# Between the attentions of a four-layer network: order of row reads, weight reads, FFN matmuls, rounding steps and key buffers

## Chip, cores and metric

One core of one Trainium2 chip. The metric is the device time of one execution in microseconds (us); a kernel is stated by the median of its runs. The engines are TensorE (PE), VectorE (DVE), ScalarE (ACT), GpSimd (POOL), and SyncE (SP), which here only issues DMAs.

## The reference, cut to what matters

A residual stream x of 2 x 1024 tokens and 128 features passes four layers, each with an attention and a feed-forward network (FFN) on the same normalised input:

```python
for L in range(4):
    xn = _layernorm(x)
    s = attention[L](xn)            # 0: grouped, rotary; 1: 16 heads; 2: features x features; 3: one shared head of keys
    g = _silu(ffn[L](xn))           # 0: mixture, top 2 of 8, capacity; 1: 8 small experts, all computed; 2: ternary; 3: mixture
    x = x + s * g

# layer 1's FFN
gate, up = einsum('td,edf->tef', xf, Wg), einsum('td,edf->tef', xf, Wu)
h = silu(gate) * up                 # then weighted by the router, and projected down, plus a shared expert

# layer 2's FFN; _tlin is x @ w.T * s with w in {-1, 0, 1}
h = silu(_tlin(x, w1_w, w1_s)) * _tlin(x, w2_w, w2_s)
h = gelu(_tlin(h, h1_w, h1_s), approximate=False)
h = gelu(_tlin(h, h2_w, h2_s), approximate=False)
return _tlin(h, w3_w, w3_s)
```

## The kernel before, in words

Matmuls that need more than one rounded product split an operand into a high part (rounded to the fast 32-bit format by an ACT cast) and a low part (what the cast left out, subtracted by DVE), and run three matmuls: high x high, low x high, high x low (`mm3`, L828). "Batch" below means such a group of matmuls into one PSUM bank.

All engines walk through one list of items, written out by hand in `whole_order` (L472), each taking from an item its own share of the work, and wait for each other by semaphores. An item that uses PSUM draws its bank from a pool in turn (`BANKS`, `POOLS`), so the order also fixes the banks. Engines are in order: an item that waits holds up all that stands behind it on its engine, and SP holds up every DMA behind a wait.

The list is, in time: attention 0 (to about 556 us of the trace), layer 0's experts (to about 660), attention 1 (to 1201), layer 1's FFN (to 1286), layer 2 (attention and ternary FFN interleaved, to 1464), attention 3 (to 2036), layer 3's experts. A `barrier` item stands where buffers change owners.

- **Experts** (`expert_order`, L370). Layer 0 has 16 units, two per expert, of 384 and 256 rows. For each unit `xrows` (SP) reads its rows into one of five xg buffers, `cols` transposes them, four `up` batches with gelu and one `down` follow; `ew` reads an expert's two weight matrices, `esplit` rounds the first. `xrows` of unit u + 3 stands ahead of unit u. `wld` reads the seven pieces of layer 1's weights (six of 256 KB, into the place of its values, `vt`) and `ald` its output matrix (512 KB, `wo`): all of them stand in front of unit 0.
- **Layer 1's FFN** (`first_ffn_order`, L422). Four chunks of 512 tokens, five tiles m of 128 hidden features. `f1g` is the gate batch with ACT's silu, `f1u` the up batch with DVE's product, `f1w` (m < 4) spreads the router's weights over the tile by two matmuls whose contraction has 8 rows, and DVE multiplies them in. `f1sp` splits the weights in pieces (gh/gl, then uh/ul), `f1wt` the router's weights (wth/wtl).
- **Layer 2** (`layer2_order`, L444). `f2g` is two batches, gate and up, into two banks. For each, ACT takes silu of the gate into one of three temporary tiles, DVE multiplies the up bank in, ACT casts the product to `hs` high, DVE subtracts to `hs` low; then `f2h 0` and `f2h 1` (hidden layers, 12 matmuls each per tile) and `f2d`. All of one `f2g` is one item, so on ACT the silu of the next tile stands behind the cast of this one. `a2g`, `a2t`, `a2s`, `a2sm`, `a2sn`, `a2n`, `a2m`, `a2f` are the steps of its attention, per batch of 1024 tokens; `aln0` to `aln2` its layer norm, where `aln2` scales eight tiles on DVE and then POOL; `sil` and `xup` update x. The list takes one entry of the attention's part and one of the FFN's in turn.

This is f2g on ACT before, with the product's wait (`emptied`) inside:

```python
S.activation(t[:], ps[:], AF.Silu, scale=fn.sc[:, mt:mt + 1]).then_inc(s.free[b], 1)
w.wait_ge(*pl.emptied(*item))
if ch:
    w.wait_ge(*pl.filled("f2h", 0, ch - 1, 3))
S.copy(fn.hs[0][0][:, mt, :].bitcast(FR), t[:]).then_inc(s.f2_act, 1)
```

- **Start of an attention** (`attention_order`, L239). The keys of the first heads come in two column halves, each: matmuls, ACT's cast into `stage[0]`, DVE's low part into `stage[1]`, DMAs from both into kA and kB (items `k`, `khi`, `klo`). The second half waits until the copies of the first have left the stage. The queries go the same way through `hq` (`qhi`, `qlo`). Then come the `max` items, score maxima that DVE reduces. Layer 3 has also `sn` and `snt`, scores of the null key, ahead of the first maxima. `early` reads the next FFN's first weights into the stage once the last key item's copies are through.

## Time and profile before

| | |
|---|---|
| median of 3 runs | 2091.08 us (2090.39 to 2096.55) |
| the profiled execution, its own time | 2092.04 us |
| its span in the profile | 2090.2 us |
| mean granted clock of TensorE | 0.954 of 2.4 GHz |
| layer 0's experts, 556 to 660 us | PE busy 79.4 of 104.0 us, clock 0.86 |
| layer 1's FFN, 1201 to 1286 us | PE busy 78.2 of 85.0 us, clock 0.84 |
| layer 2, 1286 to 1464 us | PE busy 156.3 of 178.0 us, clock 0.96 |
| attention 1, 660 to 1201 us | PE busy 514.4 of 541.0 us, clock 0.97 |

How to read it: the span runs from the first to the last instruction, and the execution's own time is 1.84 us more. "Busy" of PE counts an instruction from its start to its end, at whichever clock it ran; a stretch can be fully busy at half the clock. In a row of a timeline the square brackets hold the time for which the engine did nothing before it, and what ended that.

### The profile page before, as it was taken

To read this page: it belongs to the slowest core of one execution; us is meant where nothing else is said; L and a number is where in the kernel's file an instruction comes from. 1 tells how busy PE (TensorE), PEld (TensorE's weight loads), DVE (VectorE), ACT (ScalarE), POOL (GpSimd) and SP (SyncE) were. 2 spreads that over 40 slices of the span, in tenths; PEclk is the share of its full clock that TensorE was granted. 3 is DMA by queue.
4 is the path that set the end of the run, shared out by engine and by line. 5 is a ranking of instruction groups with operands and counts; after the bars stand their busy time and mean duration, and the time that the engine had idled before them with its cause. 6 is when DMAs were issued, how large, how long until landed. Compare 5 with 4: busy or idle time off the path is not lost.

```text
span 2090.2 us, 31314 instructions
## 1 busy us (share of the span) xinstructions
PE 1891.8 (91%) x9714; PEld 1247.0 (60%) x9714; DVE 1381.0 (66%) x3813; ACT 965.5 (46%) x2003; POOL 1230.7 (59%) x1600
## 2 busy tenths in 40 slices
PE   5899999999885899999999898988889999888985
PEld 3565556665584566666666566876556655545554
DVE  7887777777343776666666455446688888766733
ACT  2435444444454554555545434545335444444443
POOL 1668977777544367777777700011367777788743
PEclk9999999999897899999999979999799999999997
DMA  5336132132152433443444120000312223222233
GB/s 143 93 86 156 45 82 53 35 73 51 53 161 68 104 80 88 105 101 79 105 98 96 38 84 20 1 12 1 91 41 67 64 58 74 66 67 69 59 106 100
DMA packets 125966, 155.54 MB, mean 74 GB/s; under 512 B 21880, under 2 KB 66200, under 8 KB 125544
## 3 DMA queue, kind: packets, MB, share of 16 engines
q1 hardware_dynamic: 121704, 145.42, 28.1%
q0 software_dynamic: 4096, 8.12, 1.2%
q8 instruction: 78, 1.28, 0.3%
q14 instruction: 88, 0.72, 0.1%
HBM read 47.84 MB, written 17.40 MB: 31 GB/s over the span
## 4 chain that ended last, share of the span: by engine, by line
PE 59%; POOL 11%; DVE 11%; issue 11%; ACT 4%; DMA 1%; SPq 1%; POOLq 0%; DVEq 0%; ACTq 0%
PE P L826 58%; POOL acc L1583 4%; DVE P L1974 2%; POOL yd L1600 2%; POOL pr L1561 2%; POOL xg L1591 2%; POOL acc L1580 2%; ACT pr L1347 1%; DVE mx L1963 1%; DVE mx L1984 1%; DMA xg<-xs,sidx 1%; PE P L912 1%; DVE qB L1936 1%; DVE bst L1875 0%; PE P L853 0%
## 5 line engine op out<-in xcount | busy, mean ns | idle before, releaser
L1583 POOL TENSOR_TENSOR acc<-acc,pr 128x512 f32<-128x512 f32 (+3 forms) x768 | 677.0, 904 | 61.4 <-ACT pr L1347 37.1
L1347 ACT ACTIVATE pr<-P 128x512 f32<-128x512 f32 (+1 forms) x768 | 396.0, 567 | 314.5 <-PE P L826 307.5
L826 PE MATMUL P<-pr,vt 128*64 128x512 f32 (+3 forms) x2304 | 431.4, 499 | 17.6 <-POOL pr L1561 16.9
L826 PE MATMUL P<-qA,kA 128*128 128x512 f32 (+2 forms) x1024 | 395.5, 390 | 27.7 <-ACT pr L1347 23.8
L1561 POOL TENSOR_SCALAR_AFFINE_SELECT pr<-pr 128x256 f32<-128x256 f32 x384 | 156.7, 408 | 367.0 <-ACT pr L1347 261.2
L826 PE MATMUL P<-qB,kB 128*128 128x512 f32 (+2 forms) x1024 | 368.3, 366 | 0.0
L826 PE MATMUL P<-kA,qA 128*128 128x512 f32 (+2 forms) x1152 | 313.2, 374 | 17.7 <-DMA qA<-hq 4.8
L826 PEld LDWEIGHTS P<-qA,kA 128*128 128x128 f32 x1024 | 194.4, 190 | 153.2 <-issue 73.4
L1963 DVE TENSOR_REDUCE mx<-P 128x1 f32<-128x512 f32 x384 | 244.7, 683 | 57.3 <-PE P L826 55.7
L826 PEld LDWEIGHTS P<-pr,vt 128*64 128x64 f32 x2304 | 141.5, 137 | 221.1 <-issue 148.7
L826 PEld LDWEIGHTS P<-kA,qA 128*128 128x128 f32 x1152 | 194.0, 195 | 125.9 <-issue 72.0
L1974 DVE CUSTOM_DVE_ANT_0 P<-P,maskQ 128x128 f32<-128x128 f32 (+3 forms) x384 | 178.2, 519 | 102.3 <-PE P L826 101.2
L1580 POOL TENSOR_TENSOR acc<-pr,pr 128x384 f32<-128x384 f32 x192 | 217.8, 1146 | 32.6 <-ACT pr L1347 32.4
L826 PEld LDWEIGHTS P<-qB,kB 128*128 128x128 f32 x1024 | 195.1, 190 | 21.3
L1974 DVE CUSTOM_DVE_ANT_0 P<-P,maskQ,mx 128x128 f32<-128x128 f32 (+3 forms) x384 | 188.6, 553 | 11.6 <-PE P L826 9.0
L1342 ACT ACTIVATE pr<-P 128x512 f32<-128x512 f32 x192 | 86.2, 488 | 134.9 <-PE P L826 131.4
L826 PE MATMUL P<-xh,weights 128*128 128x512 f32 (+2 forms) x336 | 114.9, 425 | 9.9 <-DVE stage L1944 4.4
L2021 DVE SCALAR_TENSOR_TENSOR P<-P,rd 128x512 f32<-128x512 f32 x96 | 66.5, 693 | 81.4 <-ACT rd L1360 81.4
L1600 POOL DMA_INDIRECT yd<-y,ni x64 | 62.3, 973 | 90.2 <-DVE y L2252 67.7
L826 PE MATMUL P<-acc,ones 128*64 128x512 f32 x384 | 104.4, 622 | 8.9 <-POOL acc L1583 5.3
L1974 DVE DVE_READ_ACCUMULATOR2_ANT mx<- 128x1 f32 x768 | 107.3, 140 | 0.3
L826 PE MATMUL P<-wo,z 128*128 128x128 f32 x768 | 98.1, 282 | 7.4 <-DVE z L2028 7.4
(345 smaller groups left out, 2705.9 us busy)
## 6 DMA issues: line engine op xcount, KB each, us to landing
qA<-hq SPq DMA_DIRECT2D x384, 128.0 KB
kA<-stage SPq DMA_DIRECT2D x168, 128.0 KB
qB<-qB SPq DMA_DIRECT2D x96, 128.0 KB
kB<-stage SPq DMA_DIRECT2D x84, 128.0 KB, 2.4
nr<-null_share SPq DMA_DIRECT2D x64, 128.0 KB
yd<-in_c_zero SPq DMA_DIRECT2D x32, 128.0 KB, 2.7
w<-in_L_W SPq DMA_DIRECT2D x16, 256.0 KB, 5.7
xg<-xg SPq DMA_DIRECT2D x24, 129.0 KB
```

The source lines that it names most:

```text
L826: return P.matmul(out, lhs, rhs, start=start, stop=stop)
L912: P.transpose(ps[0:72, 0:128], m.A[L].mx[pl.chunk(*k) % 2][:], m.ident[:]).then_inc(s.full[b], 1)
L1342: S.activation(a.pr[slot][:, :, 512 - wide:512], src, AF.Exp, scale=0.125).then_inc(s.free[b], 1)
L1347: S.activation(a.pr[slot][:, r, 512 - wide:512], m.bank[b][:, 512 - wide:512], AF.Exp, scale=0.125).then_inc(s.free[b], 1)
L1561: G.affine_select(tile, tile, [[0, 2], [1, 128]], ALU.is_ge, 0.0, 0, -1).then_inc(s.sel, 1)
L1580: G.tensor_tensor(acc[:, sl], p0[:, sl], pt[:, sl], ALU.add).then_inc(s.acc, 1)
L1583: G.tensor_tensor(acc[:, sl], acc[:, sl], pt[:, sl], ALU.add).then_inc(s.acc, 1)
L1591: G.indirect_dma_start(xgd[L], bass.IndirectOffsetOnAxis(ap=r.sidx[:, i // 2, i % 2:i % 2 + 1], axis=0), r.xs[i % 2][:], None).then_inc(s. ...
L1600: G.indirect_dma_start(yd[L], bass.IndirectOffsetOnAxis(ap=e.ni[u % 4][0:wide, t:t + 1], axis=0), e.y[u % 4][0:wide, t, :], None).then_inc ...
L1963: V.reduce_max(mx[:, 8 + j:9 + j], ps[:, 0:wide], X).then_inc(s.free[b], 1)
L1974: top = V.tensor_tensor_reduce(tile, tile, m.maskQ[:, 512 - wide:512], 1.0, least, ALU.add, ALU.max, mx[:, j:j + 1])
L2021: chain(V.scalar_tensor_tensor(out=m.bank[b][:], in0=m.bank[b][:], scalar=-1.0, in1=y[:], op0=ALU.mult, op1=ALU.mult))
```

## The change

1. Layer 0's experts: `xrows` of units 2 and 3 stand ahead of the first weights, and later ones four units ahead instead of three. The seven `wld` and the `ald` of layer 1 stand one in each of units 0 to 6 (the last with `ald`).
2. Layer 1's FFN: the first chunk begins gate 0, gate 1, up 0, gate 2, up 1. At the barrier before it, ACT loads the table of activations for silu.
3. Layer 2: cast and low part of `f2g` are an item of their own, `f2c`, placed one tile later; `sil` and `xup` of layer 1's last chunk stand ahead of the first `f2g`; the attention's steps stand two entries later, and `aln2` of batch 0 behind `a2n`, `a2m` of batch 1.
4. The second key item of each attention goes through two of the buffers `z`, with semaphores of its own. Layer 3's `sn` stands behind the first maxima.

```diff
@@ attention_order @@
-    if L == 3:
-        od.add("sn", L, 0)
     for g in range(10):
...
-        if L == 3 and g == 1:
-            od.add("snt", L, 0)
+        if L == 3 and g < 2:
+            od.add(("sn", "snt")[g], L, 0)
@@ expert_order @@
+    ahead = 4 if L == 0 else 3
     if L == 0:
-        od.add("xrows", L, 2)
+        od.extend([("xrows", L, 2), ("xrows", L, 3)])
     od.extend([("ew", L, 0), ("ew", L, 1), ("esplit", L, 0), ("cols", L, 0), ("ew", L, 2)])
-    if L == 0:
-        od.extend([("wld", 1, i) for i in range(len(PIECES[1]))] + [("ald", 1)])
     for u in range(n):
-        if u + 3 < n:
-            od.add("xrows", L, u + 3)
+        if u + ahead < n:
+            od.add("xrows", L, u + ahead)
+        if L == 0 and u <= len(PIECES[1]):
+            od.add(*(("wld", 1, u) if u < len(PIECES[1]) else ("ald", 1)))
@@ first_ffn_order @@
     for ch in range(4):
+        if ch == 0:
+            od.extend([("f1g", 0, 0), ("f1g", 0, 1), ("f1u", 0, 0), ("f1g", 0, 2), ("f1u", 0, 1)])
         for m in range(5):
-            od.extend([("f1g", ch, m), ("f1u", ch, m)])
+            od.extend([it for it in (("f1g", ch, m), ("f1u", ch, m)) if it not in od.place])
@@ layer2_order @@
-    od.extend([("a2s", 0), ("f2g", 0, 0), ("f2g", 0, 1), ("sil", 1, 3), ("xup", 1, 3), ("f2g", 0, 2), ("f2g", 0, 3), ("ln1", 2, 1), ("lnr", 2, 1), ("a2sm", 0, 0), ("a2sm", 0, 1),
+    od.extend([("a2s", 0), ("sil", 1, 3), ("xup", 1, 3), ("f2g", 0, 0), ("f2g", 0, 1), ("f2c", 0, 0), ("f2g", 0, 2), ("f2c", 0, 1), ("f2g", 0, 3), ("f2c", 0, 2),
+               ("f2c", 0, 3), ("ln1", 2, 1), ("lnr", 2, 1), ("a2sm", 0, 0), ("a2sm", 0, 1),
...
-    att = [[], [("xT", 2, 2)], [("xT", 2, 3)], [("a2g", 1)], [("a2t", 1)]] + rest(0) + out(0)[:2] + [[("a2s", 1)]] + out(0)[2:] + [[("a2sm", 1, 0), ("a2sm", 1, 1), ("aln1", 0)]]
-    att += [[("a2sn", 1, 0)], [("a2sn", 1, 1)]] + scale(0) + rest(1) + [[("wld", 3, i)] for i in range(3)] + [[("nld",)]]
+    att = [[], [("xT", 2, 2)], [("xT", 2, 3)], [("a2g", 1)], [("a2t", 1)], [], []] + rest(0) + out(0)[:2] + [[("a2s", 1)]] + out(0)[2:] + [[("a2sm", 1, 0), ("a2sm", 1, 1), ("aln1", 0)]]
+    att += [[("a2sn", 1, 0)], [("a2sn", 1, 1)]] + rest(1) + scale(0) + [[("wld", 3, i)] for i in range(3)] + [[("nld",)]]
-    gate = lambda ch: [[("f2g", ch, m)] for m in range(4)]
+    gate = lambda ch: [[("f2g", ch, m)] + [("f2c", ch, n) for n in ((), (0,), (1,), (2, 3))[m]] for m in range(4)]
@@ Plan @@
+    def second_keys(self, L, b, kp, c):
+        return [x for x in self.key_items if x[0] == L].index((L, b, kp, c)) == 1
+    def key_stage(self, m, *k):
+        return m.A[k[0]].z[2:4] if self.second_keys(*k) else m.stage
@@ scalar_program @@
             if kind == "barrier":
+                if k[0] == 2:
+                    S.preload_act_table_set("silu_and_others")
...
-                w.wait_ge(*pl.emptied(*item))
+            elif kind == "f2c":
+                ch, mt = k
+                gate = ("f2g",) + k
+                t = m.F2.tmp[(od.step[gate] + 1) % 3]
+                b2, uses2, _ = od.bank[gate][1]
+                w.wait_ge(s.free[b2], uses2 + 1)
                 if ch:
                     w.wait_ge(*pl.filled("f2h", 0, ch - 1, 3))
@@ vector_program @@
+            elif kind == "f2c":
+                ch, mt = k
+                f2, n = m.F2, od.step[("f2g",) + k]
+                t = f2.tmp[(n + 1) % 3]
                 w.wait_ge(s.f2_act, n)
                 V.tensor_tensor(f2.hs[0][1][:, mt, :].bitcast(FR), t[:], f2.hs[0][0][:, mt, :], ALU.subtract).then_inc(s.f2_lo, 1)
```

Where the order moves, as it stands on the engines. On SP at the start of layer 0's experts, first before, then now (xg are rows, w and w1raw the experts' weights, vt the first pieces of layer 1's):

```order
L1636 DMA xg_105<-xg 128x2x129
L1638 DMA xg_105<-xg 128x129
L1771 DMA w_100<-in_L_W 128x4x128
L1771 DMA w_101<-in_L_W 128x4x128
L1768 DMA w1raw_89<-in_L_W 128x512
L1771 DMA w_102<-in_L_W 128x4x128
L1673 DMA vt_167<-in_L_Wq 128x512 x2
L1673 DMA vt_167<-in_L_Wk 128x512 x2
L1673 DMA vt_167<-in_L_Wv 128x512 x2
L1687 DMA wo<-in_L_Wo 128x8x128
L1636 DMA xg_106<-xg 128x2x129
```

```order
L1656 DMA xg_105<-xg 128x2x129
L1658 DMA xg_105<-xg 128x129
L1656 DMA xg_106<-xg 128x2x129
L1791 DMA w_100<-in_L_W 128x4x128
L1791 DMA w_101<-in_L_W 128x4x128
L1788 DMA w1raw_89<-in_L_W 128x512
L1791 DMA w_102<-in_L_W 128x4x128
L1656 DMA xg_107<-xg 128x2x129
L1658 DMA xg_107<-xg 128x129
L1693 DMA vt_167<-in_L_Wq 128x512
L1788 DMA w1raw_90<-in_L_W 128x512
L1791 DMA w_103<-in_L_W 128x4x128
```

The rows of unit 3 (xg_106) stood behind all reads for layer 1; now they stand ahead of every weight, those of unit 4 (xg_107) ahead of the first read for layer 1, and one such read comes with each unit.

On PE at the start of layer 1's FFN, before and now (gh, gl and uh, ul are high and low part of gate and up weights, wth and wtl the router's weights):

```order
L826 MATMUL P<-xl,gh 128x512
L826 MATMUL P<-xh,uh 128x512
L826 MATMUL P<-xh,ul 128x512
L826 MATMUL P<-xl,uh 128x512
L826 MATMUL P<-wth,selr 128x512
L826 MATMUL P<-wtl,selr 128x512
L826 MATMUL P<-xh,gh 128x512
```

```order
L839 MATMUL P<-xh,uh 128x512
L839 MATMUL P<-xh,ul 128x512
L839 MATMUL P<-xl,uh 128x512
L839 MATMUL P<-xh,gh 128x512
L839 MATMUL P<-xh,gl 128x512
L839 MATMUL P<-xl,gh 128x512
L839 MATMUL P<-xh,uh 128x512
L839 MATMUL P<-xh,ul 128x512
L839 MATMUL P<-xl,uh 128x512
L839 MATMUL P<-wth,selr 128x512
L839 MATMUL P<-wtl,selr 128x512
L839 MATMUL P<-wth,selr 128x512
```

The second fence begins after two gate batches. The first f1w, which followed the first gate and the first up batch, now follows five batches of 128 rows, and the second f1w comes right behind it.

On ACT at layer 2's start, before and now (ftmp and the two stage tiles are the temporary tiles of f2g; L1487 is its silu, L1491 its cast, now L1502 and L1511; xf is `sil`):

```order
L1487 ACTIVATE ftmp<-P,sc 128x512
L1491 CAST hs_318<-ftmp 128x512
L1487 ACTIVATE stage_15<-P,sc 128x512
L1491 CAST hs_318<-stage_15 128x512
L1440 ACTIVATE xf<-xf 128x512
L1487 ACTIVATE stage_16<-P,sc 128x512
L1491 CAST hs_318<-stage_16 128x512
L1487 ACTIVATE ftmp<-P,sc 128x512
L1491 CAST hs_318<-ftmp 128x512
```

```order
L1455 ACTIVATE xf<-xf 128x512
L1502 ACTIVATE ftmp<-P,sc 128x512
L1502 ACTIVATE stage_15<-P,sc 128x512
L1511 CAST hs_318<-ftmp 128x512
L1502 ACTIVATE stage_16<-P,sc 128x512
L1511 CAST hs_318<-stage_15 128x512
L1502 ACTIVATE ftmp<-P,sc 128x512
L1511 CAST hs_318<-stage_16 128x512
L1511 CAST hs_318<-ftmp 128x512
```

Each cast now stands behind the silu of the next tile, and `sil` ahead of them all.

## Rows read from the trace of the kernel before

**Rows 1.** The page, part 1: busy us, share of the span, instructions.

```profile
PE 1891.8 (91%) x9714; PEld 1247.0 (60%) x9714; DVE 1381.0 (66%) x3813; ACT 965.5 (46%) x2003; POOL 1230.7 (59%) x1600
```

**Rows 2.** Windows, layer 0's experts: length, busy PE, PEld, DVE, ACT, POOL, PEclk, DMA, GB/s.

```profile
580.00:585.00 5.00, 1.41 (x5) 1.41 (x6) 0.28 (x1) 0.68 (x2) 2.81 (x3) 0.57 1.09 320
585.00:590.00 5.00, 5.00 (x31) 5.00 (x31) 1.41 (x6) 2.53 (x5) 0.00 (x0) 0.75 0.57 176
```

**Rows 3.** Timeline, layer 0's experts: start, us, what; then the issue of one pair.

```profile
574.89 1.87 SPq L1636 DMA_DIRECT2D xg<-xg  x1
...
583.59 0.69 PE L1046 MATMUL P<-ident,xg 128*128 128x128 f32 x2 [5.24 <-issue]
...
vt<-in_L_Wv SPq DMA_DIRECT2D x2, 256.0 KB, 7.7
```

**Rows 4.** Timeline, first FFN: start us, us, what, idle before it and releaser.

```profile
1202.95 0.77 PE L826 MATMUL P<-xh,gh 128*128 128x512 f32 x1 [2.32 <-DVE gl L2281]
...
1205.60 0.79 PE L826 MATMUL P<-xh,uh 128*128 128x512 f32 x1 [1.03 <-DVE ul L2281]
...
1207.61 1.28 ACT L1465 ACT_TABLE_LOAD   x1
...
1208.36 0.79 PE L826 MATMUL P<-wth,selr 8*128 8x512 f32 x1 [1.12 <-DVE wtl L2286]
...
1209.51 0.80 PE L826 MATMUL P<-xh,gh 128*128 128x512 f32 x1
...
1225.00 0.63 PE L826 MATMUL P<-xh,gh 128*128 128x512 f32 x1
```

**Rows 5.** Windows, first FFN and fourth chunk of the ternary FFN.

```profile
1220.00:1225.00 5.00, 5.00 (x12) 3.02 (x11) 1.38 (x2) 1.14 (x2) 0.00 (x0) 0.50 0.01 3
1225.00:1230.00 5.00, 5.00 (x18) 3.09 (x17) 2.77 (x4) 1.19 (x2) 0.00 (x0) 0.92 0.01 2
1240.00:1245.00 5.00, 5.00 (x22) 3.13 (x21) 3.14 (x5) 2.30 (x4) 0.00 (x0) 1.00 0.00 0
1410.00:1415.00 5.00, 3.24 (x11) 1.46 (x10) 3.25 (x5) 2.64 (x5) 0.00 (x0) 1.00 0.00 0
```

**Rows 6.** Timeline, start of layer 2: fourth tile and first hidden matmuls.

```profile
1297.32 0.68 ACT L1487 ACTIVATE ftmp<-P,sc 128x512 f32<-128x512 f32 x1
...
1298.11 0.75 DVE L2317 SCALAR_TENSOR_TENSOR ftmp<-P,sc,ftmp 128x512 f32<-128x512 f32 x1
1298.89 0.62 ACT L1491 CAST hs<-ftmp 128x512 fp32r<-128x512 f32 x1 [0.89 <-DVE ftmp L2317]
...
1299.54 0.69 DVE L2320 TENSOR_TENSOR hs<-ftmp,hs 128x512 fp32r<-128x512 f32 x1 [0.68 <-ACT hs L1491]
...
1300.34 7.59 PE L826 MATMUL P<-hs,hw 128*128 128x512 f32 x24 [5.78 <-issue]
```

**Rows 7.** Timeline, second batch of layer 2's attention.

```profile
1364.53 1.16 PE L826 MATMUL P<-wvT,ab 128*128 128x129 f32 x8 [1.22 <-DVE ab L2386]
...
1368.98 2.08 DVE L1902 TENSOR_SCALAR sacc<-sacc,mv,vb 128x128 f32<-128x128 f32 x4
...
1374.57 2.05 PE L826 MATMUL P<-weights,va 128*128 128x128 f32 x8 [4.63 <-DVE va L2358]
```

**Rows 8.** Timeline, after the fourth chunk's gates.

```profile
1430.52 0.69 ACT L1510 ACTIVATE h<-P,sc 128x512 f32<-128x512 f32 x1
...
1431.26 3.02 PE L826 MATMUL P<-hs,hw 128*128 128x512 f32 x12 [2.10 <-ACT h L1510]
```

**Rows 9.** Timeline, second keys of layers 0, 1 and 3.

```profile
31.19 0.58 ACT L1305 CAST stage<-P 128x512 fp32r<-128x512 f32 x1 [3.55 <-DVE P L1928]
...
682.51 0.58 ACT L1305 CAST stage<-P 128x512 fp32r<-128x512 f32 x1 [0.57 <-DMA kB<-stage]
...
683.24 0.59 SPq L1708 DMA_DIRECT2D qB<-qB  x1
...
1473.99 1.14 PE L826 MATMUL P<-xh,weights 128*96 128x512 f32 x2 [4.44 <-DVE stage L1944]
```

More of the change, by code:

```diff
@@ L714, in signals @@
     s.zx, s.zy = {0: one("zx0"), 3: one("zx3")}, {0: one("zy0"), 3: one("zy3")}
[L715 removed]
+    s.q_dup, s.q_low, s.q_max, s.keys_a, s.keys_b = some("q_dup", 3), some("q_low", 3), some("q_max", 3), some("keys_a", 2), some("keys_b", 2)
     s.disp, s.x_rows, s.nul_in = some("disp", 2), some("x_rows_", 5), one("nul_in")
@@ L769, in weighed, with keys_copied, keys_there @@
         return self.emptied("pv", L, b, p, c, 0)
-    def keys_copied(self, n):
-        heads = sum(1 if x[0] == 3 else 2 for x in self.key_items[:n])
+    def keys_copied(self, n, second=False):
+        heads = sum(1 if x[0] == 3 else 2 for x in self.key_items[:n] if self.second_keys(*x) == second)
         return 32 * heads, 16 * heads
-    def keys_there(self, L, b, h, part):
-        return self.keys_copied(self.od.nth("khi", L, b, h // 2 if L != 3 else 0, part))
+    def keys_there(self, s, L, b, h, part):
+        item = L, b, h // 2 if L != 3 else 0, part
+        second = self.second_keys(*item)
+        upper, lower = self.keys_copied(self.od.nth("khi", *item), second)
+        return (s.keys_a[second], upper), (s.keys_b[second], lower)
     def key_item_before(self, L, b, kp, c):
@@ L1299, in run @@
                 src = m.bank[od.bank[("k",) + k][-1][0]]
-                if pl.key_item_before(*k):
+                if pl.key_item_before(*k) and not pl.second_keys(*k):
                     w.wait_ge(*pl.emptied("k", *pl.key_item_before(*k)))
-                if n > 1:
-                    w.wait_ge(s.keys_a, pl.keys_copied(n - 1)[0])
-                    w.wait_ge(s.keys_b, pl.keys_copied(n - 1)[1])
-                S.copy(m.stage[0][0:wide, :].bitcast(FR), src[0:wide, :]).then_inc(s.k_hi, 1)
+                if n > 1 and not pl.second_keys(*k):
+                    w.wait_ge(s.keys_a[0], pl.keys_copied(n - 1)[0])
+                    w.wait_ge(s.keys_b[0], pl.keys_copied(n - 1)[1])
+                S.copy(pl.key_stage(m, *k)[0][0:wide, :].bitcast(FR), src[0:wide, :]).then_inc(s.k_hi, 1)
             elif kind == "v" and k[0] == 1:
@@ L1719, in run @@
                     for slot, rows in heads:
-                        Y.dma_start(a.kA[0:64, slot, cs], m.stage[0][rows, :]).then_inc(s.keys_a, 16)
+                        Y.dma_start(a.kA[0:64, slot, cs], pl.key_stage(m, *k)[0][rows, :]).then_inc(s.keys_a[second], 16)
                 else:
@@ L1723, in run @@
                     for slot, rows in heads:
-                        Y.dma_start(a.kA[64:128, slot, cs], m.stage[1][rows, :]).then_inc(s.keys_a, 16)
+                        Y.dma_start(a.kA[64:128, slot, cs], pl.key_stage(m, *k)[1][rows, :]).then_inc(s.keys_a[second], 16)
                     for slot, rows in heads:
-                        Y.dma_start(a.kB[64:128, slot, cs], m.stage[0][rows, :]).then_inc(s.keys_b, 16)
+                        Y.dma_start(a.kB[64:128, slot, cs], pl.key_stage(m, *k)[0][rows, :]).then_inc(s.keys_b[second], 16)
             elif kind == "rows":
@@ L1941, in run @@
                 w.wait_ge(s.k_hi, od.nth("khi", *k))
-                if n > 1:
-                    w.wait_ge(s.keys_a, pl.keys_copied(n - 1)[0])
-                V.tensor_tensor(m.stage[1][0:wide, :].bitcast(FR), m.bank[b][0:wide, :], m.stage[0][0:wide, :], ALU.subtract).then_inc(s.free[b], 1)
+                hi, lo = pl.key_stage(m, *k)
+                if n > 1 and not pl.second_keys(*k):
+                    w.wait_ge(s.keys_a[0], pl.keys_copied(n - 1)[0])
+                V.tensor_tensor(lo[0:wide, :].bitcast(FR), m.bank[b][0:wide, :], hi[0:wide, :], ALU.subtract).then_inc(s.free[b], 1)
             elif kind == "v" and k[0] != 1:
```

15 lines of the change are left out of this document (7 added, 8 removed).

## The prediction

> **What bounds the kernel.** I read the page first: TensorE (PE) is busy for 1891.8 of 2090.2 us [rows 1], so a saving counts only where it takes an idle stretch, or a stretch at the lower clock, from PE. The table of windows then shows where these lie: inside the attentions PE is busy at full clock, so the change, which touches only what lies between them, has to be paid for by four short places. I went through each with the timeline of all engines, reading for every idle time of PE what ended it. "Half" and "full" below are the two levels of its clock, 1.2 and 2.4 GHz.
>
> **Layer 0's experts.** The row read of unit 3 (xg) is issued at 574.89, behind the seven reads of layer 1's weights, whose last pair lands after 7.7 us; unit 3's transposes start at 583.59, after 5.24 us of idleness [rows 3]. "Issue" as the releaser there means that the page knows no engine for it; the read is what is late. The window from 580 to 585 has a clock of 0.57 and the next 0.75 [rows 2]: PE came back at half and reached full near 587.5, so 3.8 us of work ran at half and lost 1.9 us. The change asks for unit 3's rows before any weight and puts one weight read into each unit. The row read then has only three reads of biases and unit 2's rows ahead of it. The term is 5.2 + 1.9 = **7.1 us**. What can be late next is a weight of an expert behind one more row read; a row read of 0.13 MB takes 0.4 us at the 320 GB/s of that window [rows 2], which the lower bound covers. Bounds: 4 us (another, shorter stall appears, clock falls all the same) and 8 us. The seven issues are moved, not added; SP has the time.
>
> **Start of the first FFN (layer 1).** PE stands for 1.03 us before the first up matmul (for ul) and 1.12 us before the first f1w (for wtl) [rows 4]. Now two more gate batches and one more up batch, which need neither, stand in those places: 2.15 us gone. The preloaded activation table takes 1.28 us [rows 4] out of ACT's queue ahead of the first silu; PE did not wait for that silu, so I cost it at nothing, but it is what keeps ACT ahead now: without it the banks of the first gates would come free 1.3 us later, when PE already wants them for f1w.
> The larger term is the clock. From 1209.51 to 1225.00 [rows 4] PE worked without a gap and yet at 0.50; it rose only inside the next window [rows 5], right after two gate-and-up pairs that have no f1w between them (the fifth tile of a chunk has none). Everywhere before that a pair was followed by f1w's two matmuls, which fill only 8 of 128 rows. After 583.59 the clock rose within 3.9 us of gapless full-row work [rows 2, 3]. The new order opens, at the 1202.95 of the first gate batch [rows 4], with five batches (gate, gate, up, gate, up): fifteen full-row matmuls, 6.3 us at the 12 in 5 us of the window at half [rows 5]. I take it that the clock rises 5 us into them, near 1208. From there the chunk, which without it would end at 1225.0 - 2.15 = 1222.85, has 14.9 us of half-clock work left; 12 matmuls in 5 us against 22 in the window at full clock [rows 5] make that 8.1 us, a gain of 6.8, with the waits 8.9. Against that stands that two f1w batches now come back to back, and the clock may fall for a while after them; falling and rising again as after 583.59, 3.8 us of stretch at half twice over, would cost some 4 us. Even odds on it: **7.0 us** for waits and clock. Bounds: 2.2 (it never rises earlier) and 9.5.
> The Trainium skill speaks against this reading: its page "TensorE: Matmul & The Clock Gate" (Part 1: The HAM clock gate) says that a sustained busy engine is what lifts the throttle and that the hardware doesn't count instructions. By that rule the kind of matmul would not matter and the order would bring its waits alone, 2.2 us. This trace does not agree with it: PE was gapless for 15 us at 0.50 [rows 4, 5].
>
> **Start of layer 2.** PE ends the fourth gate pair at 1294.56 and idles 5.78 us until the low part of the fourth tile is there [rows 6]. Before, each tile went silu (0.68), product (0.75), cast (0.62) in one ACT item, so that ACT stood still for the product of the same tile and the next silu waited; the sil and xup of chunk 3 were in between as well. Now the cast is its own item one tile later, and sil/xup run ahead, under the last down and a2s matmuls. Then only the last tile's own chain follows PE: its silu starts as its gate bank is done, one up batch (three matmuls, 0.7 us) before 1294.56, near 1293.9; the product ends 0.75 after the up bank, 1295.4 with the engines' gaps; cast 0.62 and subtraction 0.69 end at 1296.8. PE starts 3.5 us earlier. Its 24 matmuls took 7.59 us, because the clock had fallen; at full they would take 5.6, but the layer norm's chain of DVE and ACT behind the casts moves by 3.5 only, so I add 0.6: **4.1 us** (bounds 2.5 and 5.5).
> **Second batch of its attention.** PE waited 4.63 us for the copies of a2n, which stood on DVE behind aln2's scalings (2.08 us for four of them beside POOL), and came back at half [rows 7]. These now come later, under the hidden layer's matmuls. But a2sn(1) is now behind the product of f2g(2,0), which waits for a silu that stands behind two table loads, and a2n cannot start before it: it was 1.22 us late [rows 7], and I estimate 4 (the product's and the normalisation's 2 us on top of the old wait and more). The one stall is traded for the other: **1.0 us** (bounds -3 and 4).
> **Fourth chunk's gates and after.** PE idles 1.76 us in the window from 1410 to 1415, about 0.3 more before the next matmuls, and 2.10 at 1431.26, where it waits for a gelu that ACT could give only at 1430.52, behind two table loads and the norm [rows 5, 8]. With the casts out of the silus' way and the norm's load no longer ahead of the first silu, the banks come free about a tile sooner and the gelu some 5 us sooner. I take nearly all of the 4.2 us, **3.8 us** (bounds 1 and 5). What is late next is the low part of layer 2's last hidden tiles on DVE.
>
> **Second keys through z.** Layer 0: ACT's second cast waited for DVE's rotation sum, not for the key copies: nothing. Layer 1: it waited for the copy at 682.51, but SP is issuing copies without a break up to 683.24 and later, and the keys' copies come behind these [rows 9]: nothing. Layer 3: PE stood 4.44 us for DVE's second stage, which only frees the bank of sn [rows 9]; now the first maxima come first, and they wait for the query copies, which move by nothing, while sn's matmuls are pushed behind them: I put it at **0** (bounds -1 and +2).
>
> **The sum.** 7.1 + 7.0 + 4.1 + 1.0 + 3.8 = 23.0 us off the profiled execution's 2092.04: 2069.0. The median of the runs, 2091.08, is 0.96 below that execution: **2068.1 us**. The measurement can tell 0.3% (6.3 us) from no change.
>
> **Rivals.**
> - The clock stays at half through the first chunk, or falls back at once: the first FFN gives 2.2 instead of 7.0, 2072.9 us. For it: one sight of a rise behind pairs is little. Against: rows 2 and 5 together. 0.2.
> - Layer 2's waits are only passed on: DVE has the same work, and a2n, a2m and the norm wait in another order. The start keeps its 4.1, the second batch loses 3 and the end gains 1: 6.8 us less than forecast, 2074.9. For it: DVE and ACT have few gaps there. 0.15.
> - Slower: the weight reads, one per unit, arrive in front of row reads and starve the experts one unit after another, as unit 3 was starved: 7.1 us each time. The first term goes, and from the third such unit on (3 x 7.1 = 21.3 against the other 15.9) it is slower; with four, 2103.6. Against: already in the window from 585 to 590 the DMA share was down to 0.57, with experts' reads running [rows 2], so one more read per unit has room. 0.02.
> - The rows of layer 0's experts come no earlier, since the reads queue in another place, and the rest is refilled within each place: at most the 2.2 and 1 of plain waits, 2088, so that the change doesn't do what it says. 0.03 with what is left over. Against: the order of issue on SP, which alone delayed that read [rows 3].
> The forecast has 0.6.
>
> **How the numbers follow.** The range takes the forecast's own bounds (2061 to 2073 for most of them together) and the first two rivals: 2059 to 2078. Faster by over 0.3% is all but the last two: 0.95; within 0.3%: 0.03; slower: 0.02.
>
> **What would show it.** Right: no idle time before unit 3's transposes and a clock of 1.0 from 574 on; ul and wtl gone from PE's waits and a clock of 1.0 before 1215 in the old count; the wait before the first hs matmuls near 2.3 us; no 2 us wait for a gelu. Wrong: new waits of PE on DMA between 580 and 610; the clock at 0.5 up to the fifth tile; a wait of PE for ab above 4 us with a2m no earlier.

## The result, and the profile after

| | before | after |
|---|---|---|
| median of the timed runs | 2090.73 us (4 runs, 2087.49 to 2096.55) | 2067.63 us (4 runs, 2066.22 to 2069.05) |
| ratio | | 0.9886, 95% interval 0.9863 to 0.991 |
| the profiled execution | 2092.04 us, span 2090.2 | 2066.22 us, span 2064.4 |
| mean granted clock | 0.954 | 0.962 |

The forecast was 2068.1 us in a range of 2059 to 2078: 0.5 us off. The terms behind it did less well: one was far too small, one too large, and the clock, which differs between profiles of equal work, took its part (below). In the page, PE's busy time falls by 11.7 us against [rows 1], so about half of the 25.8 us between the profiled executions is idle time of PE and half is work that ran at full clock instead of half:

```profile
PE 1880.1 (91%) x9714; PEld 1244.2 (60%) x9714; DVE 1382.7 (67%) x3813; ACT 966.3 (47%) x2004; POOL 1232.8 (60%) x1600
```

**Layer 0's experts**, against [rows 2, 3]: two windows, then PE's first transposes of unit 3 and SP's issue of the rows of unit 6 ahead of a read for layer 1. The transposes have no bracket: PE did not wait.

```profile
575.00:580.00 5.00, 5.00 (x45) 4.97 (x44) 1.50 (x9) 2.65 (x8) 0.00 (x0) 1.00 1.11 331
580.00:585.00 5.00, 5.00 (x41) 5.00 (x40) 2.54 (x9) 3.60 (x9) 3.25 (x3) 1.00 1.09 336
```

```profile
579.12 0.46 SPq L1656 DMA_DIRECT2D xg<-xg  x1
579.45 0.38 PE L1059 MATMUL P<-ident,xg 128*128 128x128 f32 x2
579.62 1.48 SPq L1693 DMA_DIRECT2D vt<-in_L_Wk  x1
```

**First FFN**, against [rows 4, 5]: windows, then PE's timeline. The waits for ul and wtl are gone. A matmul of 512 columns follows the one before after 0.42 us up to 1199.31 and after 0.23 us from 1199.61 on: the clock rose 5.5 us after the first gate batch. A later wait of 2.24 us, for a silu, was there before too.

```profile
1195.00:1200.00 5.00, 5.00 (x14) 3.42 (x12) 2.18 (x4) 3.37 (x7) 0.00 (x0) 0.56 1.02 306
1200.00:1205.00 5.00, 5.00 (x22) 3.05 (x21) 3.98 (x7) 1.93 (x5) 0.00 (x0) 1.00 1.05 357
```

```profile
1193.86 0.77 PE L839 MATMUL P<-xh,gh 128*128 128x512 f32 x1 [2.32 <-DVE gl L2302]
...
1198.89 0.63 PE L839 MATMUL P<-xl,gh 128*128 128x512 f32 x1
1199.31 0.46 PE L839 MATMUL P<-xh,uh 128*128 128x512 f32 x1
1199.61 0.39 PE L839 MATMUL P<-xh,ul 128*128 128x512 f32 x1
1199.84 0.40 PE L839 MATMUL P<-xl,uh 128*128 128x512 f32 x1
1200.17 0.49 PE L839 MATMUL P<-wth,selr 8*128 8x512 f32 x1
...
1247.32 0.79 PE L839 MATMUL P<-wth,selr 8*128 8x512 f32 x1 [2.24 <-ACT sg L1480]
```

**Layer 2**, against [rows 6 to 8]: every wait of PE of over 0.5 us between the fourth tile's gates and attention 3. The start waits 2.35 instead of 5.78; va is no longer waited for (4.63 before); the wait for ab grew from 1.22 to 1.88. Around the fourth chunk it now waits 1.92 for a silu and 2.97 for a low part.

```profile
1279.90 7.34 PE L839 MATMUL P<-hs,hw 128*128 128x512 f32 x24 [2.35 <-issue]
1343.57 1.16 PE L839 MATMUL P<-wvT,ab 128*128 128x129 f32 x8 [1.88 <-DVE ab L2411]
1387.60 7.77 PE L839 MATMUL P<-hs,hw 128*128 128x512 f32 x33 [1.92 <-ACT stage L1502]
1413.48 4.60 PE L839 MATMUL P<-hs,hw 128*128 128x512 f32 x12 [2.97 <-DVE hs L2351]
1428.16 3.81 PE L839 MATMUL P<-w,h 128*128 128x128 f32 x32 [0.98 <-ACT h L1530]
```

In the kernel before, PE's waits around that chunk were smaller and more, beside the 2.10 of [rows 8]:

```profile
1410.98 0.50 PE L826 MATMUL P<-xh,tw 128*128 128x512 f32 x1 [0.53 <-ACT ftmp L1487]
...
1413.59 0.73 PE L826 MATMUL P<-xh,tw 128*128 128x512 f32 x2 [0.78 <-ACT stage L1487]
1415.29 10.92 PE L826 MATMUL P<-hs,hw 128*128 128x512 f32 x47 [0.74 <-DVE stage L2317]
...
1443.84 3.02 PE L826 MATMUL P<-hs,hw 128*128 128x512 f32 x12 [0.56 <-DVE hs L2326]
```

The 2.97 us are DVE's: the null key of layer 3 (`null`, L2018 to L2025, 6.9 us from its first row to its last) stands ahead of the low parts. DVE in the changed kernel:

```profile
1404.75 0.68 DVE L2018 TENSOR_TENSOR weights<-weights,weights 128x512 f32<-128x512 f32 x1
...
1411.45 0.17 DVE L2025 TENSOR_TENSOR weights<-weights,weights 128x16 fp32r<-128x16 f32 x1
1411.54 0.68 DVE L2351 TENSOR_TENSOR hs<-stage,hs 128x512 fp32r<-128x512 f32 x1
1412.14 0.68 DVE L2351 TENSOR_TENSOR hs<-ftmp,hs 128x512 fp32r<-128x512 f32 x1
1412.74 0.68 DVE L2351 TENSOR_TENSOR hs<-stage,hs 128x512 fp32r<-128x512 f32 x1
```

Every kernel of this study has the same stages, so the length of a stage can be compared over all profiles. PE's timeline gives it, from the first matmul of a stage to the first of the next, in us. (Layer 2 is counted from the last down matmul of the first FFN on.)

| kernel | attention 0 | experts 0 | attention 1 | first FFN | layer 2 | attention 3 |
|---|---|---|---|---|---|---|
| before | 553.9 | 104.5 | 532.0 | 82.4 | 178.4 | 555.4 |
| after | 554.9 | 96.6 | 529.2 | 74.5 | 166.6 | 560.0 |
| x1_experts | 554.3 | 98.1 | 531.1 | 82.5 | 179.1 | 559.9 |
| x2_ffn1 | 553.1 | 103.5 | 529.2 | 74.3 | 179.0 | 554.9 |
| x3_layer2 | 554.6 | 103.9 | 528.8 | 81.3 | 166.5 | 557.2 |
| x4_keys | 554.4 | 104.0 | 531.4 | 82.5 | 178.4 | 556.0 |
| x5_rows128 | 554.5 | 104.5 | 531.7 | 75.6 | 178.7 | 555.3 |
| x6_between | 554.8 | 96.8 | 531.6 | 75.6 | 167.0 | 555.3 |
| x7_f2c | 553.2 | 105.3 | 529.0 | 76.1 | 171.4 | 557.5 |
| x8_att | 554.1 | 104.2 | 532.1 | 76.1 | 176.0 | 557.7 |
| x10_nokeys | 553.7 | 96.7 | 530.2 | 71.0 | 166.6 | 555.6 |
| x11_rows | 554.5 | 98.5 | 531.7 | 81.1 | 179.2 | 555.1 |
| x9_later | 554.7 | 96.5 | 528.8 | 70.7 | 161.6 | 558.2 |
| x12_later_nokeys | 554.9 | 99.4 | 529.1 | 70.6 | 161.6 | 555.2 |

Two things are to be seen. The stages that a part of the change touches fall into groups (experts 103.5 to 105.3, then 96.5 to 99.4). And the attentions differ by 2 to 5 us between kernels whose instructions there are the same: one profile pair can't show a term of that size in them.

### The profile page after: what moved, and what is told of

Its sections match the earlier page's. It is cut to its first block, busy times and chain, and to the rows that moved or that the text cites. A ratio compares the mean times of both kernels' runs of the same rounds, so it can differ in the third digit from the quotient of the medians.

```text
span 2064.4 us, 31306 instructions
## 1 busy us (share of the span) xinstructions
PE 1880.1 (91%) x9714; PEld 1244.2 (60%) x9714; DVE 1382.7 (67%) x3813; ACT 966.3 (47%) x2004; POOL 1232.8 (60%) x1600
## 4 chain that ended last, share of the span: by engine, by line
PE 60%; DVE 12%; POOL 12%; issue 10%; ACT 4%; DMA 2%; SPq 1%; POOLq 0%; DVEq 0%; ACTq 0%
PE P L839 58%; POOL acc L1603 4%; POOL yd L1620 3%; DVE P L1995 2%; POOL pr L1581 2%; POOL acc L1600 1%; POOL xg L1611 1%; ACT pr L1362 1%; DVE mx L1984 1%; DVE mx L2005 1%; DMA xg<-xs,sidx 1%; PE P L925 1%; DVE qB L1956 1%; PE P L866 0%; DVE bst L1895 0%
## 5 line engine op out<-in xcount | busy, mean ns | idle before, releaser
L839 PE MATMUL P<-kA,qA 128*128 128x512 f32 (+2 forms) x1152 | 313.8, 375 | 26.7 <-DMA qA<-hq 11.8
L839 PE MATMUL P<-acc,ones 128*64 128x512 f32 x384 | 105.3, 627 | 8.9 <-POOL acc L1603 5.3
```

The source lines that it names most:

```text
L839: return P.matmul(out, lhs, rhs, start=start, stop=stop)
```

## Experiments

### The four parts, each alone

x1_experts is before with the expert part of the diff:

```diff
-        od.add("xrows", L, 2)
+        od.extend([("xrows", L, 2), ("xrows", L, 3)])
-        od.extend([("wld", 1, i) for i in range(len(PIECES[1]))] + [("ald", 1)])
+        if L == 0 and u <= len(PIECES[1]):
+            od.add(*(("wld", 1, u) if u < len(PIECES[1]) else ("ald", 1)))
```

> Only the change in layer 0's experts (row reads of units 2 and 3 ahead of the weights, one read for layer 1 per unit). Theory, from the two traces: the row read alone held unit 3, and with it goes the stretch at half clock behind it: about 8 us off the kernel before (between the first transposes and the last expert's matmuls the changed kernel gained 8.0), no idle time before unit 3's transposes. Rival A: only the plain wait of 5.2 us goes and the clock falls elsewhere: 5 us. Rival B: part of it comes from what the other parts do (semaphores, buffers): 3 us or less.

Measured: 2083.55 us against 2090.16 of before beside it, ratio 0.9969 (0.9957 to 0.998); 6.6 us, with an interval of 4.2 to 9.0. That alone would not tell the theory (8) from rival A (5). The profile does: the experts take 98.1 us, there is no wait before unit 3's transposes, and the clock is full from 574 to the last expert's matmuls, so it did not fall elsewhere.

x2_ffn1 has the first FFN's part:

```diff
+        if ch == 0:
+            od.extend([("f1g", 0, 0), ("f1g", 0, 1), ("f1u", 0, 0), ("f1g", 0, 2), ("f1u", 0, 1)])
+                if k[0] == 2:
+                    S.preload_act_table_set("silu_and_others")
```

> Only the change at the start of layer 1's FFN (five batches before the first f1w, table loaded at the barrier). Theory of the clock: 8.5 us off the kernel before, as the changed kernel gained between its first gate batch and 1266; granted clock 1.00 from about 10 us after the first gate batch on, against 25 us before. Rival (the order brings only its waits, and the clock rises for another reason): 2.2 us, and a clock at half up to the fifth tile.

Measured: 2082.82, ratio 0.9964 (0.9951 to 0.9977); 7.3 us. The clock was full 5.4 us after the first gate batch. The rival, 2.2, is outside the interval (0.9977 is 4.8 us).

x3_layer2 has the layer 2 part:

```diff
+    gate = lambda ch: [[("f2g", ch, m)] + [("f2c", ch, n) for n in ((), (0,), (1,), (2, 3))[m]] for m in range(4)]
+    att += [[("a2sn", 1, 0)], [("a2sn", 1, 1)]] + rest(1) + scale(0) + [[("wld", 3, i)] for i in range(3)] + [[("nld",)]]
...
```

> Only layer 2 (f2c as its own item, sil and xup first, attention's steps two entries later, aln2 moved). Theory, from the traces: 11.5 us off the kernel before (3.1 at the start, 8.2 from there to the barrier). Rival (as predicted): 8.9, with the second batch worth 1 and the fourth chunk 3.8. If layer 2 gains only because the FFN before it ended at another clock: under 6.

Measured: 2078.41, ratio 0.994 (0.992 to 0.9959); 11.8 us. The rival's 8.9 is just inside that interval (8.6 to 16.7), so the stage has to decide: layer 2 took 166.5 us, 11.9 less, and that behind a first FFN in the old order, which rules out the third possibility.

x4_keys has the keys and sn:

```diff
+    def key_stage(self, m, *k):
+        return m.A[k[0]].z[2:4] if self.second_keys(*k) else m.stage
+            od.add(("sn", "snt")[g], L, 0)
```

> Only the second keys through z and sn behind the first maxima. Theory, from the traces: attention 1 gains 2.4 us between its first transposes and its 60th us, since the second cast no longer waits for the copies of the first; attention 0 nothing; attention 3 loses about 0.8 (its first key x query matmul waits 5.6 us for a copy where the old order waited 4.4 for DVE): 1.6 off the kernel before. Rival (as predicted): 0, and the 2.4 us in attention 1 come from what stands on SP or DVE behind the experts. Second rival: the 2.5 us that attention 0 and the 3 us that attention 3 took longer in the changed kernel belong to this part and not to chance: it is then 3 us slower.

Measured: 2091.37, ratio 1.0009 (0.9997 to 1.0021), no difference that can be told from noise: the interval runs from 0.6 us faster to 4.4 slower, so the second rival, 3 us slower, is not excluded by it. What the expectation took for a gain in attention 1 was none: x2_ffn1, whose attention 1 is that of before, has it as well. Windows there of before, of x2_ffn1 and of x4_keys (length, busy PE, PEclk, DMA, GB/s):

```profile
685.00:690.00 5.00, 4.67 (x15) 0.65 0.87 203
690.00:695.00 5.00, 4.29 (x11) 0.50 0.41 93
```

```profile
685.00:690.00 5.00, 4.41 (x13) 0.66 0.78 180
690.00:695.00 5.00, 4.26 (x16) 1.00 0.03 2
```

```profile
685.00:690.00 5.00, 3.40 (x12) 1.00 0.86 200
690.00:695.00 5.00, 3.44 (x12) 1.00 0.23 53
```

Between short waits the clock is at half in one profile and full in another. The profile of before shows a slow start of attention 1.

The four medians add up to 6.6 + 7.3 + 11.8 - 1.2 = 24.5 us; together the parts gave 23.1. Within the intervals they add.

### What holds the clock down in the first FFN

x5_rows128, on the kernel before; it leaves out the router's weighting of the first chunk:

```diff
-                mm(ps[:], f.selr[:, mt, :].bitcast(FR), f.wth[:, tk].bitcast(FR), True, False)
+                lh, rh, rl = (f.gh[:, mt * 128:mt * 128 + 128], m.xh[:, tk], m.xl[:, tk]) if ch == 0 else (f.selr[:, mt, :], f.wth[:, tk], f.wtl[:, tk])
+                mm(ps[:], lh.bitcast(FR), rh.bitcast(FR), True, False)
```

> The kernel before, but in the first chunk of layer 1's FFN the two matmuls of each f1w multiply the gate weights (128 rows) with xh and xl instead of the router's weights (8 rows) with selr; they fill the same bank, take 512 columns each and wait for the same things. So the router's weighting of that chunk is left out. Theory of the clock (matmuls of 8 rows between the others hold it at half): it rises within some 7 us of the start of the gapless stretch at 1209.5, before 1217 instead of at 1226, and the kernel gains 4 to 5 us. Rival (the kind of matmul does not matter): half clock up to 1225, time unchanged within 1 us.

Measured: 2083.34 against 2089.5, ratio 0.9967 (0.9954 to 0.998); 6.2 us faster, with an interval of 4.2 to 9.6. PE still waited 0.97 for ul and 1.45 for wtl; its windows:

```profile
1205.00:1210.00 5.00, 2.65 (x5) 0.50 0.99 326
1210.00:1215.00 5.00, 5.00 (x17) 0.70 1.07 365
1215.00:1220.00 5.00, 5.00 (x26) 1.00 0.30 96
```

The clock rose 4.0 us into the gapless stretch (at 1213.0), 9.7 us after the first gate batch, where in the profile of before it took 17 (from the first f1w at 1208.36). But this one profile shows nothing by itself: x7_f2c and x8_att below keep the 8-row matmuls and rose 9.4 and 9.2 us after the first gate batch. What counts is the median. The edit also changed more than the rows. Around an f1w the matmuls of before start 0.55 to 0.60 us apart, though the profile shows no idle time, and elsewhere 0.43:

```profile
1211.81 0.63 PE L826 MATMUL P<-xl,uh 128*128 128x512 f32 x1
1212.36 0.79 PE L826 MATMUL P<-wth,selr 8*128 8x512 f32 x1
1212.96 0.62 PE L826 MATMUL P<-wtl,selr 8*128 8x512 f32 x1
1213.51 0.80 PE L826 MATMUL P<-xh,gh 128*128 128x512 f32 x1
1214.11 0.63 PE L826 MATMUL P<-xh,gl 128*128 128x512 f32 x1
```

In x5_rows128 they start 0.43 apart throughout. By these steps the four f1w of the chunk are worth 2.1 us at most without any change of the clock (an estimate: 0.6 us for each of three, 0.3 for the first, all at half). The rival, with this added, is still below the interval, so replacing the 8-row matmuls does bring the clock up earlier on the whole. Whether the 8 rows themselves hold it down, or the wider steps around them, or the other operands, no run separates. By the rule of the Trainium skill's "TensorE: Matmul & The Clock Gate" (Part 1: The HAM clock gate), as the prediction applied it, the clock of this kernel would have been that of before, and no more than the 2.1 us would have come off; the medians do not agree with that.

x6_between, on the changed kernel:

```diff
-            od.extend([("f1g", 0, 0), ("f1g", 0, 1), ("f1u", 0, 0), ("f1g", 0, 2), ("f1u", 0, 1)])
+            od.extend([("f1g", 0, 0), ("f1g", 0, 1), ("f1u", 0, 0), ("f1w", 0, 0), ("f1g", 0, 2), ("f1u", 0, 1)])
```

> The changed kernel, but the first f1w stands between up 0 and gate 2, and the second behind up 1, so that again no more than three batches come without one. Theory of the clock: the rise comes later, not before the fifth tile, some 20 us after the first gate batch, and 4 to 6 us of the changed kernel's gain of 7 in this place are lost: near 2073. Rival (only the missing waits mattered): the clock rises as in the changed kernel, 2067.6 within 1.5, or 1 us more if the first f1w waits for wtl again.

Measured: 2069.23, ratio 0.9899 (0.9882 to 0.9916). A miss for the theory as I had put it, and within what the rival gave: PE waited 0.93 for wtl and ran gate 2 and up 1 at half, and then the clock rose, 9.3 us after the first gate batch and behind a single pair:

```profile
1200.00:1205.00 5.00, 4.07 (x9) 0.50 1.05 352
1205.00:1210.00 5.00, 5.00 (x21) 0.99 0.78 270
```

The profiles of the seven kernels with the old order show that a single one proves little here. From the first gate batch to the rise of the granted clock it took 22.9 (before), 22.7 and 23.0 us (x1, x4), 19.3 and 19.2 (x3, x11), but 9.4 and 9.2 in x7_f2c and x8_att, where the clock rose behind the second pair. In x3 and x11 it rose behind the fourth pair, ahead of the fifth tile. So even with 8-row matmuls after every pair a pair can lift the clock. After an early rise the first FFN takes 76.1 us and not 81 to 82.5. With five batches in a row the clock rose within 4.1 to 5.9 us in all five profiles (after, x2, x9, x10, x12). By the stage's length the 74.4 us of after and x2 are 7.6 below the five with a late rise and 1.7 below the two with an early one.

That this varies from one execution to the next is the simplest reading, but it is not shown. The four kernels that ran together, x5 to x8, all rose early in their profiles, and those with the old order that ran at other times all rose late. If the time of the runs were the cause, before too would have been some 6 us faster beside these four. Its median there was 2089.5 us, against 2090.2 and 2091.0 at the other times.

The new order has its own fall. In x9_later and x12_later_nokeys (below) the clock fell again for 3.4 us behind the first three f1w, two of which stand back to back, while PE had no idle time. Windows of x9_later (length, busy PE, PEclk, DMA, GB/s):

```profile
1200.00:1205.00 5.00, 5.00 (x16) 0.69 1.06 362
1205.00:1210.00 5.00, 5.00 (x19) 0.97 0.19 57
```

It had risen at 1198.5, was at half from 1201.9 to 1205.3, and rose again. That costs 1.7 us. In after, x2 and x10, with the same order, it stayed full.

### Layer 2's two halves

x7_f2c is x3_layer2 with the attention's steps as before (the two empty entries behind `a2t` of batch 1 are gone too). x8_att is x3_layer2 with the old start and each cast directly behind its product:

```diff
-    att += [[("a2sn", 1, 0)], [("a2sn", 1, 1)]] + rest(1) + scale(0) + [[("wld", 3, i)] for i in range(3)] + [[("nld",)]]
+    att += [[("a2sn", 1, 0)], [("a2sn", 1, 1)]] + scale(0) + rest(1) + [[("wld", 3, i)] for i in range(3)] + [[("nld",)]]
```

```diff
-    gate = lambda ch: [[("f2g", ch, m)] + [("f2c", ch, n) for n in ((), (0,), (1,), (2, 3))[m]] for m in range(4)]
+    gate = lambda ch: [[("f2g", ch, m)] + [("f2c", ch, m)] for m in range(4)]
```

> Of the layer 2 part only f2c as its own item and the order at the start (sil and xup first); the attention's steps and aln2 stand as before. Theory: 3.1 at the start stay; in the second batch the wait for va (4.6 us) stays, since aln2 is ahead of a2n on DVE; the small waits there and in the fourth chunk go: 5 to 6 us off the kernel before. Rival (the split is all of it): 12. Second rival (nothing but the start): 3.

> Of the layer 2 part only the attention's steps two entries later and aln2 of batch 0 behind a2n and a2m of batch 1; every cast stands directly behind its product and the start is as before. Theory: the wait of 4.6 us for va goes with the clock that fell behind it, 6 us off the kernel before, the start gives nothing. Rival (the two need each other, since without the split the silus come as late as before): 3 or less.

Measured: x7_f2c 2081.03 against 2089.5, ratio 0.9964 (0.9952 to 0.9977), layer 2 171.4 us, that is 7.0 less than before: somewhat more than the theory, far from the 12 of its rival, and 3.7 of it at the start. x8_att 2088.16, ratio 0.9993 (0.9982 to 1.0004), layer 2 176.0, 2.4 less: the theory's 6 us did not come, the rival holds. (In both profiles the first FFN had its early rise, 6 us that belong to neither part.) PE's waits, first of x7_f2c, then of x8_att:

```profile
1350.88 1.16 PE L827 MATMUL P<-wvT,ab 128*128 128x129 f32 x8 [1.22 <-DVE ab L2396]
...
1360.06 2.05 PE L827 MATMUL P<-weights,va 128*128 128x128 f32 x8 [4.30 <-DVE va L2368]
...
1415.22 8.46 PE L827 MATMUL P<-hs,hw 128*128 128x512 f32 x36 [2.41 <-ACT h L1516]
```

```profile
1359.02 2.09 PE L827 MATMUL P<-wvT,ab 128*128 128x129 f32 x8 [3.25 <-DVE ab L2396]
...
1406.75 8.41 PE L827 MATMUL P<-hs,hw 128*128 128x512 f32 x29 [2.88 <-ACT stage L1488]
...
1433.47 4.62 PE L827 MATMUL P<-hs,hw 128*128 128x512 f32 x12 [2.27 <-DVE hs L2336]
```

The later steps alone remove the wait for va and bring a longer one for ab, and the two late ones in the fourth chunk. The split alone leaves va. Together they give 11.8, which is 2.4 more than the sum of 7.0 and 2.4: with the split, ab is waited for 1.88 only, 1.4 us less than in x8_att. There DVE, on its way from the product to a2sn, waits for the cast and subtracts the low part:

```profile
1355.73 0.75 DVE L2323 SCALAR_TENSOR_TENSOR stage<-P,sc,stage 128x512 f32<-128x512 f32 x1 [1.06 <-ACT stage L1488]
1357.16 0.69 DVE L2330 TENSOR_TENSOR hs<-stage,hs 128x512 fp32r<-128x512 f32 x1 [0.68 <-ACT hs L1497]
1357.89 0.42 DVE L2394 TENSOR_REDUCE sm<-ab 64x4 f32<-64x256 f32 x1
```

The other 1.0 us of the 2.4 is not traced.

### Rows or weights

x11_rows, on the kernel before:

```diff
-        od.add("xrows", L, 2)
+        od.extend([("xrows", L, 2), ("xrows", L, 3)])
-        if u + 3 < n:
-            od.add("xrows", L, u + 3)
+        if u + ahead < n:
+            od.add("xrows", L, u + ahead)
```

> The kernel before with the row reads of layer 0's experts ahead (units 2 and 3 before the weights, then four units ahead), but all reads for layer 1 still in front of unit 0. Theory (the row read of unit 3 alone was late): the experts' stage takes 97 to 98 us as with the whole edit, against 103.5 to 105.3 in the kernels with the old order, and 7 us come off. Rival (spreading the weights is what helps, since the third and fourth expert's weights stand behind them): a new wait of 2 us or more for w or w1raw between 590 and 615, and 3 us or less off.

Measured: 2082.66 against 2091.0, ratio 0.9961 (0.9949 to 0.9973). The experts take 98.5 us; one wait for rows of 0.70 us is left, at 583.96, and none for a weight. The rival, 3 us or less, is outside the interval (5.6 to 10.7). Asking for the rows first is nearly all of it; by the stage, 98.5 us against a mean of 97.4 with the whole edit, spreading the weights is worth about 1 us.

### Keys once more, and what was late next

x10_nokeys takes the keys and sn back out of the changed kernel:

```diff
-        return m.A[k[0]].z[2:4] if self.second_keys(*k) else m.stage
+                    for slot, rows in heads:
+                        Y.dma_start(a.kA[0:64, slot, cs], m.stage[0][rows, :]).then_inc(s.keys_a, 16)
```

> The changed kernel with the keys and sn as they were before. Theory (the second keys through z are worth nothing, what the attentions differ by is the clock): within 1.5 us of the changed kernel's 2067.6, either way. Rival 1 (the new buffers serve the start of attention 1): 2 to 3 us slower. Rival 2 (they cost in attentions 0 and 3): 2 to 5 us faster.

Measured: 2064.13 against 2091.0, ratio 0.9878 (0.986 to 0.9895); that interval and the changed kernel's overlap. Its first FFN was 3.5 us shorter than the changed kernel's although the order there is the same: after the wait of 2.25 us for a silu at 1246 its clock stayed full, where the changed kernel's fell (0.72 and 0.60 in the windows from 1245 to 1255). Of the twelve kernels with this wait it is the only one whose clock did not fall there.

x9_later is the changed kernel with three steps later:

```diff
-    att += out(1) + [[("aln1", 1)], []] + scale(1) + [[("wsp", 3, i)] for i in range(3)] + [[("null", 3)]]
+    att += out(1) + [[], [], [("aln1", 1)], []] + scale(1) + [[("wsp", 3, i)] for i in range(3)]
-                ("f2h", 1, 3, 0): [("xT", 3, 0)], ("f2h", 1, 3, 1): [("xT", 3, 1)]}
+                ("f2h", 1, 3, 0): [("xT", 3, 0)], ("f2h", 1, 3, 1): [("xT", 3, 1), ("null", 3)]}
-                od.extend([("ln1", 2, 0), ("lnr", 2, 0)])
+                od.extend([("ln1", 2, 0)])
-                od.extend([("ln2", 2, 0)])
+                od.extend([("lnr", 2, 0), ("ln2", 2, 0)])
```

> The changed kernel with three steps that need not be done where they stand put later: the null key (6.7 us of DVE) behind xT 3 1, where DVE has 8.8 us without work; aln1 of batch 1 two entries later, so that ACT's change of tables comes after the last silus of the fourth chunk; lnr of layer 2's first half behind the gate of tile 2 instead of tile 1 in the last chunk of the first FFN. Theory: the waits of PE at 1387.60 (1.92, for a silu), 1413.48 (2.97, for a low part) and part of that at 1247.32 (2.24, for a silu) go, with half a clock stretch each time: 4 to 7 us off the changed kernel, near 2062. Rival (each wait comes back at the next thing that is late): within 2 us of the changed kernel.

Measured: 2058.13 us (2054.49 to 2058.37), ratio 0.9843 (0.9827 to 0.9858). It is 9.5 us below the changed kernel by the medians and 9.0 by the two ratios, more than the 4 to 7 expected, and the rival is out. All of PE's waits of over 0.5 us from the middle of the first FFN to attention 3:

```profile
1276.38 7.34 PE L839 MATMUL P<-hs,hw 128*128 128x512 f32 x24 [2.35 <-issue]
1340.55 1.16 PE L839 MATMUL P<-wvT,ab 128*128 128x129 f32 x8 [0.74 <-DVE ab L2411]
1418.10 3.81 PE L839 MATMUL P<-w,h 128*128 128x128 f32 x32 [0.98 <-ACT h L1530]
1424.92 0.69 PE L839 MATMUL P<-xh,weights 128*64 128x512 f32 x2 [3.01 <-DVEq L1867]
```

The waits of 1.92, 2.97 and 2.24 are gone and none took their place. Layer 2 went from 166.6 to 161.6 us; its start took 1.5 more, because the clock was at half from 1266.8 to 1270.2, and the rest 6.5 less. The first FFN went from 74.5 to 70.7, although its clock fell once more near its start (above). By stages that is 5.0 + 3.8 = 8.8 us: the three waits are 7.1 of it and the shorter wait for ab (1.88, now 0.74) 1.1; stretches at half clock went in some places and came in others.

x12_later_nokeys is that kernel with the diff of x10_nokeys.

> The version with the null key, aln1 and lnr later, and with the keys and sn as they were before. Theory (the second keys through z are worth nothing, apart from chance of the clock): within 1.5 us of 2058.1, the median of the same version with them. Rival (they cost 1 to 4 us, as the medians of two pairs so far could be read: 1.2 slower added alone, 3.5 faster taken out): 2054 to 2057.

Measured: 2061.5 us against 2094.2 of before beside it, ratio 0.9843 (0.9823 to 0.9864), the same ratio as with the new keys. The expectation, within 1.5 us of 2058.1, is missed by the median, 3.4 above. But before, too, ran 3.2 us slower beside this kernel than beside x9_later, so the ratios are to be compared, not the medians. Adding or removing the keys has now been tried in three pairs (with them 1.2 us slower, 3.5 slower or 1.7 by the ratios, and the same), and none shows an effect beyond its interval.

## Why the prediction was right, and where it was wrong

- **Layer 0's experts, 7.1 us.** Right, mechanism and size: a mean of 104.3 us over the seven profiles in the old order, 97.4 over the six in the new one (after, x1, x6, x9, x10, x12). In none of the six did PE wait for a read of weights, so the worry about a weight behind a row read had nothing in it.
- **First FFN, 7.0 us.** Right in size (7.3 for the part alone), and the 8-row matmuls do hold the clock back on the whole (x5, by its median). "I take it that the clock rises 5 us into them" came true, at 5.5. One step was too simple: that without the new order the clock stays at half until two pairs stand together. It did in three of seven profiles; in two it rose just ahead of the fifth tile, and in two behind the second pair. So the price is 7.6 or 1.7 by the stage, and not one number. The fall of the clock after two f1w in a row, which I gave even odds and some 4 us, showed in two of the five profiles (x9, x12) and cost 1.7 us there.
- **Start of layer 2, 4.1 us.** The wait came to 2.35 us, forecast near 2.3; the stretch from the last down matmul to the first hidden one is 3.4 us shorter in the kernels with the split, and 1.9 in x9 and x12, whose clock fell in it. The 0.6 for clock came to 0.25 (24 matmuls in 7.59, now 7.34), since the clock still fell.
- **Second batch, 1.0 us.** This is the step that failed. "The one stall is traded for the other": the wait for a2sn's ab was put at 4 us, and was 1.88, only 0.66 more than before. The stretch from the 25th hidden matmul to the end of a2n is 8.2 us shorter (69.9 to 61.6), with the same matmuls in it. PE's idle time there fell by 5.3 us, from 7.2 (of which 4.63 for va) to 1.9; most of the rest is the clock, which in before was at half behind the wait for va [rows 7] and in the changed kernel is full throughout. The term names this clock but has no price for it. Why the wait for ab is short shows beside x8_att, where cast and low part stand directly behind the product of f2g(2,0) and DVE comes to a2sn after both: 3.25 us. With the cast an item of its own, DVE goes from the product straight to a2sn, and the wait for the cast (0.68) and the low part (0.69) fall out, which is the difference to 1.88. The prediction had the product in the way, rightly, but its rows give 1.22 + 2 = 3.2, and the rest of the 4 is its "and more"; nor did it say what the split, part of the same change, does at this place.
- **Fourth chunk, 3.8 us.** Also wrong: it gave nothing. The waits of the 4.2 us did go, the 2.10 for a gelu among them, but others came in their place, so that nothing was left of "I take nearly all of the 4.2 us". The sentence after the term, on what is late next (the low parts on DVE), held: 2.97 us, behind the null key's 6.9 us of DVE. The other, 1.92 for a silu behind aln1's table, was not foreseen. The stretch from a2n to attention 3 took 85.8 us before and 85.9 after, with 8.7 and 8.9 us of idle time. x9_later, which moves just these two steps later here, takes 78.9. Together this term and the one before were put at 4.8 and gave 8.1.
- **Keys, 0.** No run speaks against it. A gain is excluded by x4 beyond 0.6 us; a cost of up to 4 us is not, by any of x4, x10 and x12.
- **Not in the sum:** by the table of stages attention 0 took 1.0 us more, attention 1 2.8 less and attention 3 4.6 more. Equal instructions spread as widely in the other kernels, so these numbers show no effect.

In the two profiles the touched stages gave 7.9 + 7.9 + 11.8 = 27.6 us, 4.6 more than the sum of 23.0, and the attentions took 2.8 back. (Layer 3's experts, not in the table, took 1.7 less.) Over the medians, where chance weighs less, the parts alone are worth 6.6, 7.3, 11.8 and -1.2. What was under-priced is layer 2, by 3 us; that the total hit within 0.5 us is luck as far as that goes: the parts' medians add up to 24.5, and the whole measured 23.1.
